# Layer two of a two-layer gated attention kernel: the maximum of one score bank in four is subtracted by VectorE instead of TensorE

## The reference

```
q, k, v: 16 heads of 8 channels from layernorm(x) and ctx
scores = einsum('bhtd,bhsd->bhts', q, k) * 8 ** -0.5      # causal and padding mask
attn   = softmax(scores, axis=-1)
out    = einsum('bhts,bhsd->bhtd', attn, v) @ Wo.T + bo
x      = x + tanh(g) * out
```

## Time and profile before

| what | before |
|---|---|
| median of 3 runs | 1671.57 us (1671.38 to 1672.91) |
| span of the profiled execution | 1668.5 us |
| TensorE busy | 1592.5 us, 95% |
| VectorE busy | 1206.6 us, 72% |
| ScalarE busy | 1079.6 us, 65% |
| GpSimd busy | 1179.4 us, 71% |

### The profile page before, as it was taken

The page is one execution under the profiler, slowest core; times in us unless marked ns, Lnnn a source line. Parts: engine busy times, 40 slices in busy tenths (PEclk is TensorE's granted clock), DMA queues, the critical chain, the costliest instruction groups (busy, mean ns, idle before and its releaser), DMA issues.

```text
span 1668.5 us, 50902 instructions
## 1 busy us (share of the span) xinstructions
PE 1592.5 (95%) x15977; PEld 1386.3 (83%) x15978; DVE 1206.6 (72%) x3915; ACT 1079.6 (65%) x2725; POOL 1179.4 (71%) x1715
## 2 busy tenths in 40 slices
PE   6999999976999899999999999999999999999996
PEld 4777777756998689888988988888988988898885
DVE  3677777753554568788887888788888888787785
ACT  3777777743555556666666666666666666666654
POOL 3556656642455578887888888887888888887785
PEclk9999999987999999999999999999999999999998
DMA  2322222234542100000000000000000000000000
GB/s 74 109 73 74 76 75 76 80 96 129 146 134 77 29 17 11 17 17 21 14 18 17 17 18 16 17 16 21 14 18 17 18 17 17 16 16 11 5 8 10
DMA packets 92101, 68.95 MB, mean 41 GB/s; under 512 B 13936, under 2 KB 87696, under 8 KB 91920
## 3 DMA queue, kind: packets, MB, share of 16 engines
q1 hardware_dynamic: 76512, 49.34, 10.1%
q0 software_dynamic: 5120, 12.62, 2.4%
q10 hardware_dynamic: 10288, 4.74, 1.1%
HBM read 35.74 MB, written 22.52 MB: 35 GB/s over the span
## 4 chain that ended last, share of the span: by engine, by line
PE 81%; DVE 5%; issue 5%; POOL 5%; DMA 2%; SPq 1%; ACT 1%; POOLq 0%; DVEq 0%; ACTq 0%
PE s_bank L1884 14%; PE s_bank L1885 12%; PE s_bank L1886 12%; PE po L1702 6%; PE tb L1685 5%; PE po L1831 4%; PE s_bank L1819 4%; PE s_bank L1665 3%; PE s_bank L2034 2%; PE m L1639 1%; PE s_bank L2021 1%; PE tb L1884 1%; POOL sorted_in L652 1%; POOL qkv L726 1%; PE m L1935 1%
## 5 line engine op out<-in xcount | busy, mean ns | idle before, releaser
L726 POOL TENSOR_TENSOR qkv<-qkv,scaled 128x384 f32<-128x384 f32 x480 | 490.1, 1021 | 128.8 <-ACT scaled L1009 91.2
L1009 ACT ACTIVATE scaled<-s_bank,wg 128x384 f32<-128x384 f32 x449 | 257.2, 582 | 128.8 <-PE s_bank L1886 127.3
L1884 PE MATMUL s_bank<-proj_hi,hn_hi 128*128 128x384 f32 x900 | 331.4, 368 | 1.3 <-DVE qkv L1451 1.0
L1451 DVE SCALAR_TENSOR_TENSOR qkv<-s_bank,wg,qkv 128x384 f32<-128x384 f32 x449 | 274.2, 611 | 49.6 <-PE s_bank L1886 37.9
L1885 PE MATMUL s_bank<-proj_lo,hn_hi 128*128 128x384 f32 x900 | 303.7, 337 | 0.0
L1886 PE MATMUL s_bank<-proj_hi,hn_lo 128*128 128x384 f32 x900 | 302.1, 336 | 0.0
L869 ACT ACTIVATE pT<-tb 128x512 f32<-128x512 f32 x256 | 152.2, 595 | 148.9 <-PE tb L1685 81.3
L1884 PEld LDWEIGHTS s_bank<-proj_hi,hn_hi 128*128 128x128 f32 x900 | 169.4, 188 | 16.3 <-ACT scaled L1009 5.9
L1885 PEld LDWEIGHTS s_bank<-proj_lo,hn_hi 128*128 128x128 f32 x900 | 170.0, 189 | 3.0
L1886 PEld LDWEIGHTS s_bank<-proj_hi,hn_lo 128*128 128x128 f32 x900 | 169.0, 188 | 0.0
L1685 PE MATMUL tb<-ident,prob 128*128 128x128 f32 x1024 | 157.6, 277 | 4.8 <-ACT pT L869 4.8
(11 more groups left out here) (291 smaller groups left out, 3816.2 us busy)
## 6 DMA issues: line engine op xcount, KB each, us to landing
xs<-sorted_in SPq DMA_DIRECT2D x71, 128.5 KB, 2.1
kx<-kT SPq DMA_DIRECT2D x256, 32.0 KB, 1.9
sorted_out<-yo SPq DMA_DIRECT2D x71, 64.0 KB, 1.6
xin<-in_x SPq DMA_DIRECT2D x32, 128.0 KB
cin<-in_ctx SPq DMA_DIRECT2D x32, 128.0 KB
ctx_cols<-xcT SPq DMA_DIRECT2D x32, 128.0 KB
w<-in_L_ffn_W SPq DMA_DIRECT2D x16, 256.0 KB
xcT<-ctx_cols SPq DMA_DIRECT2D x32, 128.0 KB, 2.9
```

Of the source, the lines that this page charges most:

```text
L726: g.tensor_tensor(into, into, scaled[m % SCALED][:, 0:cols], ALU.add).then_inc(dense_added, 1)
L1009: ins = act.activation(into, bank[:, 0:3 * D], ACT.Copy, scale=wg[v % 4][:, 1, k:k + 1])
L1451: v.scalar_tensor_tensor(out=acc, in0=bank[:, 0:3 * D], scalar=wg[w % 4][:, 0, k:k + 1], in1=acc, op0=ALU.mult, op1=ALU.add).then_inc(dens ...
L1884: pe.matmul(bank[:, 0:cols], hi[:, tile], of(proj_hi), start=True, stop=False)
```

## The change

For bank 3 of every unit in layer two the matmul with `minus_ident` is gone. VectorE gets a new instruction, `diff_bank`, right behind the four maxima: it subtracts the broadcast maximum from the bank and writes the difference into `prob[3]` in SBUF. ScalarE's exponential of bank 3 then reads and writes `prob[3]`. Banks 0, 1 and 2 are as before. The counts of `max_ready` go from four to five per unit, those of `scores_ready` from four to three.

```diff
-SUBTRACTED = (1, 0, 2, 3)
+SUBTRACTED = (1, 0, 2)
...
             def exp_bank(v, j):
...
+                    if j in SUBTRACTED:
+                        act.wait_ge(q["scores_ready"], 3 * v + SUBTRACTED.index(j) + 1)
+                        wait(act, q["probT_in_psum"], 4 * v - 3 + j)
+                        shifted_scores = s_bank[j][:, :]
+                    else:
+                        act.wait_ge(q["max_ready"], 5 * v + 5)
+                        shifted_scores = flat_prob
+                    act.activation(flat_prob, shifted_scores, ACT.Exp, scale=SCALE).then_inc(q["exp_ready"], 1)
...
+            def diff_bank(w):
+
+                if exists(w):
+                    q = s[1]
+                    v.wait_ge(q["max_ready"], 5 * w + MAXIMA.index(3) + 1)
+                    wait(v, q["probT_in_psum"], 4 * w)
+                    v.tensor_tensor(prob[3][:, :, :, :].rearrange("p t r k -> p (t r) k"),
+                                    s_bank[3][:, :].rearrange("p (a k) -> p a k", k=LEN),
+                                    bcast(mx[:, 3, :], LEN, 2), ALU.subtract).then_inc(q["max_ready"], 1)
...
                 max_bank(u + 2, 3)
+                diff_bank(u + 2)
                 if u != 0:
                     take(u, "q", 1)
...
             def subtract_bank(v, j):
...
-                    pe.wait_ge(s[1]["max_ready"], 4 * v + MAXIMA.index(j) + 1)
+                    pe.wait_ge(s[1]["max_ready"], 5 * v + MAXIMA.index(j) + 1)
...
                 tokens_parts(u, 0, 2)
-                subtract_bank(u + 2, 3)
                 tokens_parts(u, 0, 3)
```

More of the change, by code:

```diff
@@ L953, in exp_bank @@
                     q = s[1]
[L954 to L957, removed]
+                    flat_prob = prob[j][:, :, :, :].rearrange("p t r k -> p (t r k)")
+                    if j in SUBTRACTED:
[6 more added lines that the diff above has]
+                    act.activation(flat_prob, shifted_scores, ACT.Exp, scale=SCALE).then_inc(q["exp_ready"], 1)
             def copy_hidden(v):
@@ L1548, in _ @@
                 max_bank(0, j)
+            diff_bank(0)
             first_stats(1, 2, 0)
@@ L1552, in _ @@
                 max_bank(1, j)
+            diff_bank(1)
             add_residual(1, 0, 0, x3[0][:, :, :])
```

## The result

| | before | changed |
|---|---|---|
| median | 1671.63 us (1671.38 to 1672.91, 4 runs) | 1679.42 us (1678.20 to 1682.49, 4 runs) |
| ratio | | 1.0049, 95% interval 1.0035 to 1.0063 |
| span of the profiled execution | 1668.5 us | 1680.8 us |
| its own time | not recorded | 1682.49 us |

The changed kernel is 0.49% slower (+7.8 us), where 0.28% (+4.7 us) was predicted; the 1679.42 us lie at the upper edge of the range. The profiled execution was the slowest of the four. Its time lies 1.7 us above its own span, so the 3.1 us that the prediction put between span and median of before were not all of one execution.

The account below looks back on a forecast made before the run. TensorE, busy throughout steps 2 to 28, was taken as the bound. 4.3 us there, -0.4 in steps 0 and 1, +0.3 in step 29, -0.2 and +0.7 in the prologue gave +4.7: median 1676.3 us, range 1672 to 1679.5.

Parts of the forecast that it names:

- The mechanism of the step: Steps 2 to 28: subtraction delays the takes, TensorE waits 0.37 us for 0.21 us saved, each step 0.16 us longer.
- The copy row: Profile row of a 128x512 copy from PSUM at 0.69 us, used to price the new subtraction at 0.69 us.
- The cheaper hand-over: Between takes of parts 1 and 2: 0.03 us instead of 0.11, +2.2 us, in all 1674.2; chance 0.18.
- The whole matmul won: All steps: take of part 2 finishes in time, 0.21 us won per step, -5.8 us, 1665.8; chance 0.05.
- Free hand-overs: VectorE's chain: dependent instructions start 0.08 us before the predecessor ends, -3.4 us in all, 1668.2; chance 0.07.
- Transposes held longer: Ahead of part 4: transposes' waits add up, with 0.40 us +0.28 us a step, about 1679.5; chance 0.08.
- GpSimd doesn't hold the subtraction: Denies the rival that GpSimd holds VectorE's subtraction, +0.6 us a step, 16 us more, 1692; chance 0.03.
- Prologue, steps 0 and 1, and step 29: Outside steps 2 to 28: prologue unit 0 -0.2 us, unit 1 +0.7, steps 0 and 1 -0.4, step 29 +0.3.
- the sum: Whole kernel: 4.3 - 0.4 + 0.3 - 0.2 + 0.7 = +4.7 us, 0.28% slower.
- 27 x 0.16 = +4.3: Steps 2 to 28, taken as 27 alike steps: each 0.16 us longer, +4.3 us together.
- the term of 0.3 us: Step 29: load of part 4 at 1564.80 instead of 1564.53, +0.3 us.

Follow-up runs that it names:

- the last experiment: Changed kernel with 40 more one-column MEMSETs at the head of VectorE's queue: 1677.09 us, ratio 1.0037 against the kernel before.
- e8: Kernel before with the change in prologue units 0 and 1 only, run a second time on a faster chip: 1674.87 us, ratio 1.0012.
- the repeat: The changed kernel itself, unedited, measured once more: 1678.95 us, ratio 1.0039 against the kernel before.
- e1: Kernel before with the change in prologue units 0 and 1 only, on the slower chip: 1771.11 us, ratio 1.0005.
- e11: The changed kernel itself, unedited, measured once more beside the kernels with fillers: 1678.95 us, ratio 1.0039 against the kernel before.
- e12: Changed kernel with 40 more one-column MEMSETs on VectorE right behind its first instruction: 1677.09 us, ratio 1.0037 against the kernel before.

## Why the prediction was right or wrong

**The mechanism of the step was right.** Where the prediction had the subtraction 0.02 us behind the maxima and 0.69 us long, it starts 0.04 us behind them and takes 0.690 to 0.693 us in all 32. The take of part 2 starts 0.10 us after part 1, where 0.11 were said. The wait before part 4 is 0.30 us, where some 0.3 were said, in each of the 28 steps 2 to 29. The ordinary step is 34.19 to 34.21 us over the six profiles of this order of the steps on chips of normal speed, +0.16 to +0.19 for +0.16.

The copy row against the cycle table of the Trainium skill, "VectorE: DVE Perf Modes", section on the TRN2 errata: the measured 0.691 us sides with the row (0.69), and not with the 0.66 us that come out of the table's entry for a PSUM source.

**The rivals are out.** The cheaper hand-over needed 0.03 us between the takes of part 1 and part 2, and it is 0.10. The whole matmul won needed part 4 without a wait. Free hand-overs, as the same page has them in its section on the DRAIN, would show a take of part 2 that starts before part 1 ends; it starts 0.10 us after. Transposes held longer: their loads start 0.05 us after the take of part 1 (1129.38 + 0.61 to 1130.04), and part 4 follows the take, not them. GpSimd doesn't hold the subtraction, whose 32 durations lie within 3 ns.

**Prologue, steps 0 and 1, and step 29 were right to 0.2 us** in a profile without a clock drop: -0.3 for -0.2, +0.7 for +0.7, -0.4 for -0.4. In step 29 of the kernel of the last experiment part 4 is loaded at 1573.64, 5.81 us after the scores (1567.83), for 1564.53 - 1559.01 = 5.52 before: +0.3 for +0.3.

**The step that failed is the sum.** It came to +4.7 us, and the same pieces came to +6.4 in a profile without a clock drop ahead of the drain, and to +11.7 in the first one. One of its terms was too small, one can't be judged, and one was missing:

- "27 x 0.16 = +4.3" treats the steps as alike. They measured +5.5 us, and +5.5 to +6.0 over the other profiles. Without two odd steps it would have been 4.2 us; another 1.3 us came in these two (35.27 and 34.47 us for 34.19), in which a delay at a place in VectorE's queue meets `res` and the adds of GpSimd. The prediction named this hold beside GpSimd, but for the subtraction and for L1347. Delays of this kind were there before the change, as the rows of before show; two more VectorE records a step only moved them onto `res`.
- The piece from the last scores to the end took 0.9 us more for the 0.3 predicted. 0.4 us of it stand ahead of a drop of the clock that every profile has in the drain. The rest goes with where that drop falls. In e8, whose kernel is that of before from step 0 on, the piece is 110.83 us, 1.3 us longer than before. The stretches of this drop in before, in e8 and in the changed kernel start 87.0, 89.7 and 90.0 us behind the last scores, and TensorE has 5.52, 7.79 and 8.04 us of work in them:

```profile
1646.10:1656.30 10.20, 5.52 (x15) 4.09 (x16) 3.75 (x12) 2.24 (x8) 0.72 (x1) 0.50 0.04 13
1652.20:1662.40 10.20, 7.79 (x20) 5.89 (x21) 3.41 (x11) 2.53 (x9) 0.72 (x1) 0.50 0.04 13
1659.80:1670.00 10.20, 8.04 (x20) 6.01 (x21) 3.15 (x11) 2.79 (x10) 0.73 (x1) 0.50 0.05 15
```

So this piece doesn't show that the term of 0.3 us was wrong.

**The missing term is TensorE's clock.** In the profiled execution the drop cost 4.1 us, in the repeat 2.4 us, in others nothing. The prediction looked at the granted clock in steps 2 to 28 only, costed the prologue's gap as its own length and so put the clock there at nothing. How often it falls with and without the change isn't settled: e1 and e8, with the change in the prologue alone, stand at 1.0005 and 1.0012 with intervals that reach to no change at one end and to +2.7 and +4.3 us at the other. The distance between +6.4 us and the +7.8 us of the first medians (+5.8 and +6.0 us in e11 and e12) is within their intervals; how much of it is the clock isn't known. That the median came out inside the range is in part luck: the range reached up for held transposes, which the runs rule out, and not for odd steps or the clock.

## What to carry to other kernels

Before moving work onto an engine that has idle time, look for its next result that the bound engine waits for: 0.69 us ahead of the takes lost some 0.17 us a step, and the same instruction behind one take won 0.17 us. Count also what a short instruction can set off by being in the queue at all. Steps that look alike in the profile of before need not stay alike, so after such a change list the length of every step and look at the odd ones first. Where the effect is a few microseconds, compare from a point behind the part that the change doesn't touch.

## What was not expected of the hardware

- At numbers 128 apart in VectorE's records (numbers 3876, 4004 and 5668 in the changed kernel, 4900, 5028, 5156 and 5668 before) an instruction or a wait starts 0.35 us late, without anything that the profile shows it to wait for (0.54 us before the statistics for 0.19). Not each such number shows it. What the delay costs depends on the instruction that it meets: 1.04 us in step 9 (35.25 us for 34.21), nothing to be seen in others (34.01 us in step 25 before, with the row at 1436.38).
- A VectorE instruction with all operands in SBUF took 1.21 to 1.25 us for 0.47 us when it started just behind the start of a GpSimd add, and ended 0.28 to 0.29 us after that add; the subtraction and L1184, L1420, with an operand in PSUM, kept their time within 3 ns.
- In the prologue TensorE was granted 0.52 of its clock over 10.7 us, behind an idle time of 0.59 us; with the same idle time the same kernel in another execution fell 10 us later, and the one with 40 more VectorE instructions not at all.
- One chip ran the same kernel in 1770.84 us for 1672: 53 us of it lie ahead of layer two's first scores, at a granted clock of 0.93 for 0.96, and in the steps the first maximum waits 3.0 us on average for 1.27.
